# Three edits to the attention stage of a two-layer network: one instruction for both products of the rotation, another order of the last part of P, and VectorE for the low weights of the second attention

## The reference

```
x = (h - mu) * rsqrt(var + EPS) * ln_g + ln_b            # 2 x 512 tokens, 256 wide
q = rope(x @ wq.T + bq)    # 16 heads of 128;  rope(x) = x * cos + x_rot * sin
k = rope(x @ wk.T + bk)
v = x @ wv.T + bv
attn = softmax(causal(q k^T / sqrt(128)))
out = (attn v) @ wo.T + bo + residual
```

## Time and profile before

| | |
|---|---|
| runs | 588.29 us median of 3 (587.86 to 592.12) |
| profiled execution | span 586.2 us; the page gives no other time of it |
| TensorE, VectorE | 535.4 us (91%), 479.2 us (82%) |
| ScalarE, GpSimd | 386.5 us (66%), 382.2 us (65%) |
| granted TensorE clock | 0.987 on the mean |
| chain that ended last | TensorE 58%, VectorE 17%, ScalarE 7%, GpSimd 5%, issue 6% |

### The profile page before, as it was taken

How to read it: one execution, slowest core, us unless ns; L and a number is a source line. 1 busy time by engine, 2 the same in 40 slices (tenths; PEclk the granted TensorE clock), 3 DMA queues, 4 the chain that set the end, 5 groups by cost and what they waited for, 6 DMA issues and landing times.

```text
span 586.2 us, 11450 instructions
## 1 busy us (share of the span) xinstructions
PE 535.4 (91%) x4186; PEld 363.1 (62%) x4186; DVE 479.2 (82%) x949; ACT 386.5 (66%) x843; POOL 382.2 (65%) x333
## 2 busy tenths in 40 slices
PE   7569999999999999999897898899999999999895
PEld 3246666566666666666565554465688778756573
DVE  7989998999999988899997787577627796767656
ACT  4476869688877787767677856666676556556231
POOL 1767988899999798978688469732223454434432
PEclk9789999999999999999999999999999999999998
DMA  8234554547664243572433824022110000000002
GB/s 296 73 82 105 104 114 100 107 104 123 101 144 86 58 80 73 119 170 55 72 64 73 207 73 139 7 72 73 51 37 1 2 1 2 0 1 1 1 2 73
DMA packets 98457, 44.64 MB, mean 76 GB/s; under 512 B 88288, under 2 KB 90720, under 8 KB 98400
## 3 DMA queue, kind: packets, MB, share of 16 engines
q1 hardware_dynamic: 97408, 43.35, 33.2%
q10 hardware_dynamic: 992, 0.55, 0.3%
HBM read 21.86 MB, written 1.05 MB: 39 GB/s over the span
## 4 chain that ended last, share of the span: by engine, by line
PE 58%; DVE 17%; ACT 7%; issue 6%; POOL 5%; POOLq 0%; ACTq 0%; DVEq 0%
PE bank L1573 51%; PE bank L1753 5%; POOL qkl L583 2%; DVE parts L1170 2%; DVE nmax L1139 2%; DVE turned L1150 1%; DVE ol L1184 1%; DVE vl L1178 1%; DVE turned L1152 1%; ACT bank L745 1%; PE bank L1617 1%; POOL rr L579 1%; ACT vh L772 1%; DVE stats L1003 1%; DVE turned L1350 1%
## 5 line engine op out<-in xcount | busy, mean ns | idle before, releaser
L1573 PE MATMUL bank<-xTh,w_all_h 128*128 128x512 f16 (+2 forms) x392 | 130.3, 332 | 5.5 <-DVE xT L1070 2.4
L1573 PE MATMUL bank<-xTl,w_all_h 128*128 128x512 f16 (+2 forms) x392 | 130.0, 332 | 0.0
L1573 PE MATMUL bank<-xTh,w_all_l 128*128 128x512 f16 (+2 forms) x392 | 129.8, 331 | 0.0
L583 POOL TENSOR_TENSOR qkl<-turned,qkh 128x512 f16<-128x512 f32 (+1 forms) x44 | 54.6, 1240 | 98.3 <-ACT qkh L870 98.1
L550 POOL TENSOR_TENSOR rr<-turned 64x512 f32<-64x512 f32 x63 | 87.4, 1387 | 29.9 <-DVE turned L1152 25.8
L745 ACT ACTIVATE bank<-bank,nmax 128x128 f32<-128x128 f32 (+3 forms) x128 | 64.1, 501 | 47.8 <-DVE nmax L1139 47.4
L560 POOL TENSOR_TENSOR qkl<-rr,qkh 128x512 f16<-128x512 f32 x64 | 75.9, 1190 | 24.5 <-ACT qkh L767 22.1
L551 POOL TENSOR_TENSOR rr<-turned 64x512 f32<-64x512 f32 x63 | 82.7, 1312 | 3.7
L870 ACT ACTIVATE qkh<-turned 128x512 f16<-128x512 f32 (+1 forms) x44 | 27.6, 628 | 59.0 <-DVE turned L1350 59.0
L1170 DVE SCALAR_TENSOR_TENSOR parts<-bank,rscaled,parts 128x128 f16<-128x128 f32 (+3 forms) x128 | 64.1, 544 | 0.2 <-ACT parts L756 0.2
L1139 DVE TENSOR_REDUCE nmax<-bank 128x1 f32<-128x128 f32 (+3 forms) x128 | 57.3, 481 | 5.8 <-PE bank L1617 4.8
(11 more groups left out here) (226 smaller groups left out, 1483.3 us busy)
## 6 DMA issues: line engine op xcount, KB each, us to landing
stage<-in_per_head SPq DMA_DIRECT2D x16, 512.0 KB, 4.2
xa<-in_codes SPq DMA_DIRECT2D x32, 128.0 KB, 2.8
stage<-in_packed SPq DMA_DIRECT2D x12, 256.0 KB, 3.1
stage<-in_scales SPq DMA_DIRECT2D x12, 256.0 KB, 4.2
pT<-parts SPq DMA_TRANSPOSE x128, 2.8
stage<-in_w1T SPq DMA_DIRECT2D x2, 512.0 KB, 4.1
x<-in_x SPq DMA_DIRECT2D x4, 128.0 KB, 2.4
rope<-in_ropes ACTq DMA_DIRECT2D x1, 512.0 KB, 7.1
```

What stands on the lines that cost most here:

```text
L583: pool.tensor_tensor(il[n % 2][0:rows, :], inter[0:rows, n % 2, :], ih[n % 2][0:rows, :], ALU.subtract).then_inc(g_il, 1)
L1573: last = pe.matmul(dst, l, r, start=start and i == 0, stop=stop and i == 2, skip_group_check=skip)
```

## The change

Five edits. (a) `rotate` makes both products in one instruction of 1,024 columns, which reads the bank twice by a broadcast. (b) The last part of P, high half on ScalarE and low half on VectorE, moves behind the rounding and the rotation of the keys. (c) The low halves of the two `w1` pieces are made by VectorE like those of the heads; GpSimd's `low_w`, its waits, and ScalarE's scaled copy go. (d) `lut_halves` moves from step 26 to the first network, behind its second product. (e) `signed` comes one step after `unpacked`.

```diff
+UNPACKED_AT = (DONE + 3, DONE + 7)
...
-            def low_w(j):
-                pool.wait_ge(a_wh, j + 1)
-                pool.tensor_tensor(w_low(j), stage[:, j % 4, :], w_high(j), ALU.subtract).then_inc(g_wl, 1)
-
...
-                pieces = [j for k in range(-2, u - 1) for j in LOWS_AT.get(k, ()) if j >= HEADS]
-                pool.wait_ge(g_wl, len(pieces))
...
-                for j in LOWS_AT.get(s, ()):
-                    if j >= HEADS:
-                        low_w(j)
...
-                last = act.activation(w_high(j), stage[:, j % 4, :], ACT.Copy, scale=W_SCALE)
-                if j >= HEADS:
-                    last = act.activation(stage[:, j % 4, :], stage[:, j % 4, :], ACT.Copy, scale=W_SCALE)
-                last.then_inc(a_wh, 1)
+                act.activation(w_high(j), stage[:, j % 4, :], ACT.Copy, scale=W_SCALE).then_inc(a_wh, 1)
...
                     high_v(s)
-                    for q in range(TPB):
+                    for q in range(TPB - 1):
                         high_p(s, q)
                 if there(s + 1):
                     high_qk(s + 1, 1)
+                if there(s):
+                    high_p(s, TPB - 1)
...
                 for j in LOWS_AT.get(s, ()):
-                    if j < HEADS:
-                        for half in halves:
-                            half_low_w(j, half)
+                    for half in halves:
+                        half_low_w(j, half)
...
-                dve.scalar_tensor_tensor(out=turned[:, p, 2 * w, :], in0=qk_bank(u, w)[:, :], scalar=bias, in1=rope[:, 0, :],
-                                         op0=ALU.add, op1=ALU.mult)
-                dve.scalar_tensor_tensor(out=turned[:, p, 2 * w + 1, :], in0=qk_bank(u, w)[:, :], scalar=bias, in1=rope[:, 1, :],
+                both = qk_bank(u, w)[:, :].unsqueeze(1).broadcast_to([P, 2, S])
+                dve.scalar_tensor_tensor(out=turned[:, p, 2 * w:2 * w + 2, :], in0=both, scalar=bias, in1=rope[:, :, :],
                                          op0=ALU.add, op1=ALU.mult).then_inc(d_rope, 1)
...
                 if there(s):
-                    for q in range(TPB):
+                    for q in range(TPB - 1):
                         low_p(s, q)
                 if there(s + 2):
                     rotate(s + 2, 1)
+                if there(s):
+                    low_p(s, TPB - 1)
...
-                if s == UNITS - 6:
-                    lut_halves()
...
-                if s in POWER_AT:
-                    unpacked(POWER_AT.index(s))
-                    signed(POWER_AT.index(s))
+                for pair in range(2):
+                    if s == UNPACKED_AT[pair]:
+                        unpacked(pair)
+                    if s == UNPACKED_AT[pair] + 1:
+                        signed(pair)
...
+                if m == 1:
+                    lut_halves()
...
-            pe.wait_ge(g_wl, lows_before(W_PIECES)[1])
+            lows_done(W_PIECES - 1)
```

More of the change, by code:

```diff
@@ L221, in sandwich @@
         s_pT = [sem(f"s_pT{q}") for q in range(TPB)]
-        g_wl = sem("g_wl")
         s_w = [sem(f"s_w{i}") for i in range(4)]
@@ L327, in of_head @@
             return [a[:, h, o:o + n] for a in (w_all_h, w_all_l)]
-        def lows_before(j):
-            return min(j, HEADS), max(j - HEADS, 0)
         def q_piece(j):
@@ L436, in load_w @@
                 if j >= 4:
[L437 to L440, removed]
+                    sp.wait_ge(d_wl, j - 3)
                 src = per_head[j] if j < HEADS else w1_dram[:, j - HEADS, :]
@@ L481, in _ @@
                     sp.dma_start(lut_row[:, :], lut.partition_broadcast(P)).then_inc(s_lut, 16)
-                    by_dve, by_pool = lows_before(W_PIECES)
-                    sp.wait_ge(d_wl, by_dve)
-                    sp.wait_ge(g_wl, by_pool)
+                    sp.wait_ge(d_wl, W_PIECES)
                     for j in range(4):
@@ L1599, in lows_done @@
             def lows_done(j):
[L1601 to L1604, removed]
+                pe.wait_ge(d_wl, j + 1)
             def scores(u, q):
```

## The result

Twelve runs of the changed kernel have a median of 586.68 us (584.64 to 588.33), twelve of the kernel before on the same chip 589.59: ratio 0.9945, interval 0.9921 to 0.9969. That is 0.55% faster where 1.4% was forecast, outside the range (576.8 to 584.2). The profiled spans are 583.5 and 586.2: the change brought 2.7 us of the 8.5.

What follows compares the result with a forecast made beforehand. TensorE was taken to bound ordinary attention steps, VectorE late ones. Savings of 1.1 (start), 2.1 (steps 3 to 20), 1.6 (two long steps) and 3.7 (steps 23 to 30), together 8.5, gave 579.8 us; range 576.8 to 584.2.

Steps and rivals of the forecast that it cites:

- (a): Rotation's two products in one instruction: 1.19 us to the next start instead of 1.32, 0.13 saved per rotation.
- (b): Keys ahead of the last part of P: 0.1 us saved in each of eight ordinary steps, 0.6 at 34.71 us.
- (c): Low halves of w1 on VectorE, 0.69 us each: both long steps fall from 9.86 to 9.05, 1.6 saved.
- (d): Table's halves leave step 26, where they took 2.8 us; under 1 us and free behind the feed-forward network's second product.
- (e): Second half of unpacking one step later: 0.5 us saved in steps 25 and 29 each; the last falls where VectorE idles.
- GpSimd's rotation can start 0.8 earlier: In attention steps, with keys ahead of the last part of P, GpSimd starts 0.8 us earlier at no cost.
- rival 4: VectorE's four new w1 halves each blocked behind a GpSimd rotation (1.74 us): two steps last 11.1, time 584.0; 7%.
- TensorE's floor in a step: Ordinary attention step: TensorE works 8.89 of 9.05 us and is the bound, leaving a hole of 0.16 at most.
- Rival 6: The loops have no further bound: eight residual steps gain 0.1 us each, late steps reach TensorE's 8.9; 577.8; 10%.
- A transposing DMA counted as covered: Each head's fourth leaves 1.2 us later, lands 2.8 after issue; its reader comes some 7 us into the step.
- The 0.6 to spare for the last low part of P: It ends 0.65 us after the scores begin; the last rows' scores, reusing its bank, begin 1.3 after.
- Feed-forward networks: 0: In the sum of the forecast, the feed-forward networks were to gain or lose nothing.

Runs made afterwards that it cites:

- e2: Kernel before with only the last part of P moved behind the keys on ScalarE and VectorE: 592.13 us, ratio 1.0044.
- e6: Changed kernel, GpSimd's rotation also waiting for the last low part of P in 9 of 32 steps (2, and 24 to 31): 582.62 us, ratio 0.9877.
- e7: Changed kernel, GpSimd's rotation also waiting for the last low part of P in all steps: 578.09 us, ratio 0.9799.
- e12: e7 with the table's halves back in step 26 and the second half of the unpacking back behind the first: 581.76 us.
- e8: Changed kernel with the second half of the unpacking back behind the first, in steps 25 and 29: 588.08 us, ratio 0.9967.
- e9: Kernel before with the last part of P behind the keys, and GpSimd's rotation waiting for the last low part of P in all steps: 587.51 us, ratio 0.9972.
- e3: Kernel before with only both products of the rotation in one instruction: 588.71 us, ratio 0.9983.
- e4: Changed kernel with VectorE's instructions with two SBUF inputs placed between the keys' rotation and the last low part of P: 584.62 us, ratio 0.9919.
- e5: Changed kernel with the old order (last part of P, then keys) in 9 of 32 steps (2, and 24 to 31): 582.8 us, ratio 0.9871.
- e1: Changed kernel with the last part of P back ahead of the keys on both engines: 586.32 us, ratio 0.9934.

## Why the prediction was wrong, point by point

- **The step that failed is (b) on VectorE**: "GpSimd's rotation can start 0.8 earlier, which costs nobody." It costs VectorE's next instruction, where that has two SBUF inputs, some 0.6 in all steps but those in which GpSimd also adds the residual. I had priced what moved (P, keys, the DMAs) and for each who waits for it, but not the instruction behind them, which did not move. e2 shows the loss with nothing else changed, e6 and e7 its end with nothing but GpSimd's start changed: 586.68 to 578.09, 8.6 us (7.3 between the profiles).
- **The rule was at hand.** The prediction names the lock, but weighed it only where instructions were added (part (c), rival 4 with 7%), not where two engines' order flips. What the prediction reads from the median of the earlier trace rows ("most don't") was true of an order in which VectorE started first, and I carried it over into one in which it doesn't: 0.69 forecast, 1.18 measured as the mean of the four new halves.
- **TensorE's floor in a step was put too high.** I took its 8.89 of busy time in the earlier trace rows as the bound. But ahead of the scores (of step 18, at 195.11) the next start came 0.38 behind the last one, where it is 0.06 in the changed kernel (at 220.41); of these 0.33 more, the profile showed 0.16 as idle and the rest as the last product running out. Back to back a step takes 8.72, and so part (b) brings up to 0.33 per ordinary step, not 0.1. The chain of the changed kernel has no hole in such a step, from the scores at 211.69 to those at 220.41 (the 63 products from 213.70 run into its first block, and nothing stands as "issue" between them):

```profile
213.70 7.04 PE bank L1556 x63
220.74 0.06 PE bank L1597
```

- This error and the first have opposite signs. With GpSimd second the time is 578.1, and 579.8 was forecast. That this is so near is in part luck: up to the scores of step 31 e7 wins 2.7 more than the forecast (table), and 1.2 that was priced at nothing is lost behind them. Rival 6 (no further bound, 577.8) was the nearest to e7.
- **A transposing DMA counted as covered was not always**: 0.97 of waiting in step 24 of the changed kernel, none before (under *e6*). The 0.6 to spare for the last low part of P held: TensorE waits for it nowhere in the changed kernel.
- **A slip in the range**: it is said to leave out the worst of rival 4, but that rival's 584.0 lies below its end, 584.2. It changes nothing here.
- **(a) held**: 1.28 long in the mean, the next starts 1.19 later. **(c) held in kind**: no instruction of 2.13 is left on GpSimd, the long steps fell to 9.25 and 9.20 (9.05 forecast); with the halves unhindered, in e7, they are at 8.88 and 8.72.
- **(d) held in its place**: the table's halves take 0.68, beside an idle GpSimd, and the product behind them still waits for ScalarE. VectorE in order of time, answering to the earlier trace rows:

```profile
339.12 0.34 DVE L1303 TENSOR_SCALAR lut_own<-lut_row 64x8 f32<-64x8 f32 x2
339.49 0.17 DVE L1306 CAST lut_h<-lut_own 128x8 f16<-128x8 f32 x1
339.70 0.17 DVE L1308 TENSOR_TENSOR lut_rest<-lut_own,lut_h 128x8 f32<-128x8 f32 x1
...
342.37 0.69 DVE L1329 SCALAR_TENSOR_TENSOR turned<-bank,turned 128x512 f32<-128x512 f32 x1 [1.37 <-ACT turned L840]
```

- **"Feed-forward networks: 0" missed 1.4.** Of it 0.65 comes in the network: the unpacking behind that product now meets GpSimd's multiplication by scales and its next low half, and two instructions of 0.28 take 1.19 and 1.24:

```profile
343.18 1.19 DVE L1105 TENSOR_SCALAR pT<-xT 128x256 int32<-128x256 int32 x1
344.29 1.24 DVE L1106 TENSOR_SCALAR pT<-xT 128x256 int32<-128x256 int32 x1
```

From its first start to its last end the unpacking there takes 3.35, against 2.69 before. It is a price of (d): with (d) undone, in e12, it takes 2.68 again, and in all kernels with (d) the same two instructions are long.

Another 0.64 is lost between the last scores and the low half of v behind them (4.37 before, 5.01 now). In the changed kernel it is again an instruction of (e), the second half of the last unpacking, which GpSimd's multiplication beside it stretches to 1.32, so that the maxima of the last scores wait; VectorE in order of time, behind scores that started at 315.88:

```profile
315.99 1.32 DVE L1113 SCALAR_TENSOR_TENSOR hot_more<-xT,hot_more 128x256 int32<-128x256 int32 x1
317.23 0.61 DVE L1119 TENSOR_REDUCE nmax<-bank 128x1 f32<-128x128 f32 x2
```

The prediction had put it where "VectorE idles". With (e) undone but (b) in place (e2, e8, e9, e12) 0.58 comes back in another form: VectorE's `ol` starts 1.80 behind the last scores instead of 1.22, since ScalarE's `oh` comes behind the last part of P. Only e3 and e4 have neither.

## What to carry to other kernels

When an instruction is moved, look also at the one that stays: list, for VectorE and GpSimd, which of two neighbours that both read SBUF starts first, before and after. If the wrong one would, a wait on the engine that has time (here one semaphore wait on GpSimd, 8.6 us) can be cheaper than another order (e4 584.62, e5 582.8). And take the floor of an engine from the distance between starts in a stretch without a hole, not from its busy time.

## What the runs showed of the hardware

- The stretch is paid by whoever starts second, by a margin of 0.16 to 0.5: the addition 0.68 or 1.32, GpSimd's rotation instruction 1.26 or 1.55 to 1.64. Where two such instructions of VectorE stand in a row, the outcome varies: GpSimd waited for both when it came 0.15 or 0.16 behind the first (2.25; kernel before, e1, e3, e5), but only for the first at 0.17 in e4 (1.64) and at 0.25 in e7 (1.55), and then VectorE's second took 1.75 or 1.76. What decides between the two, no run shows.
- Instructions with a single SBUF input are not free of it: the int32 shift of 0.28 took 1.19 to 1.24 beside GpSimd, and a small CAST of 0.17 took 1.28 before and 1.17 in e12. The section of the Trainium skill named above ("SBUF — State Buffer", the two separate sides) counts VectorE's two-port performance modes among what takes the pair; whether these instructions run in one, no row here shows.
- One stretch at TensorE's lower level (1.2 GHz) comes and goes between kernels that are alike there. e3 was granted 0.89 in the 3 us from 326, in which TensorE was busy for 1.78, and 0.54 in the next 3; the changed kernel had 1.00 throughout; VectorE's reading of the second half's attention sums (`nrm`) starts 18.8 behind the last scores in e3 and 17.4 in the kernel before, whose program is the same there; e1, e2 and e9 have 19.3 to 19.5, the others 17.5 to 18.1. Rows of e3: length and busy times as in the earlier trace rows, the clock third from the end.

```profile
326.00:329.00 3.00, 1.78 (x13) 1.35 (x13) 3.00 (x4) 2.79 (x4) 1.83 (x2) 0.89 1.17 166
329.00:332.00 3.00, 3.00 (x11) 1.36 (x10) 2.46 (x2) 1.33 (x2) 1.37 (x1) 0.54 0.90 241
```

- The runs of one kernel scatter with the mean granted clock: the kernel before took 585.5 to 585.9 at 0.993, 587.7 to 590.6 at 0.987, 589.7 to 592.3 at 0.984 and 590.6 to 592.6 at 0.981. A difference of 2 us needs many runs of both kernels, or the profile.
